# A linear-attention stage: u's turned rows get a tile of their own and are read back in the turn that wrote them

## The chip, the cores and the metric

The kernel runs on one core of one Trainium2 chip. The metric is device time in microseconds (us) of one execution, the median of several runs. Lower is better.

## The reference, cut to what matters

Four blocks in a row, each added to a residual x of shape (2, 2048, 256), fp32:

```python
x = x + attn_a(layernorm(x))      # gated scan
x = x + ffn(layernorm(x))         # 256 -> 1024 -> 256, ternary weights, gelu
x = x + attn_b(layernorm(x))      # the block that the change touches
x = x + ffn(layernorm(x))

# attn_b: 16 heads, q, k, v of 64 each, one step of the recurrence:
k_C  = k_t . C_QV                 # C_QV before this step
G    = G    + k_t (x) k_C
S_K  = S_K  + k_t (x) k_t
C_QV = C_QV + q_t (x) v_t
o_t  = q_t . (S_K . C_QV - G)
```

After the 2048 steps o is multiplied by W_o.

## The kernel before, in words

The program has three stages: `first_stage` (the gated scan), `feed_forward`, and `attention`, which also contains the last feed-forward (the D_ tiles) at its end. Every engine runs a fixed list of instructions written out by hand; semaphores order the engines against each other. There is no scheduler.

`attention` replaces the recurrence by a chunked form. The 2048 tokens of both batches are cut into 32 chunks of 64 tokens, and one pass of the loop `for j in range(CHUNKS)`, here called turn j, works on one chunk of all 16 heads and both batches. Turns run from 0 to 31. In a turn TensorE (PE) issues in this order:

- `by_states`, 128 products of 64x64 with the two running states (line 1261 with state_s, line 1265 with state_z). Batch 1 needs its bank back from the output of two chunks ago: it waits for `x_added`, the two adds of `add_out` on VectorE (DVE, line 1654).
- four projections of the next block (lines 256 to 258: q in even turns, k in odd ones). The first two need the banks of the masked scores free (`a_masked`).
- `o_by_scores` (1287) and `u_and_s` (1276). The latter reads k as rows (krow, `krow_done`) and the masked scores.
- `change_z` (1298) for chunk j-1. It reads u as rows (urow, `urow_done`).
- `values` (1240 to 1242), `scores_of` twice (1250: ut times q, then k times q for the next turn), and `out_product` of chunk j-1 (1310 to 1312).

The change is about the way of u from columns to rows. ScalarE (ACT) copies u to `ut`. DVE turns it in 32x32 blocks into the tile `turned` (`turn_u`, line 1627). SyncE's queue (SP) writes `turned` to a scratch tensor in device memory (`save_u`, line 1114) and reads it back in four transfers in another order of partitions into `landed` (`land_u`, line 1120). ACT copies it to `urow` (`store_u_rows`, line 1517). k takes the same way through its own tile k32 (`save_k`, `land_k`, `store_k_rows`), and so do the normalised rows of x, of which a block of 256 tokens of each batch is needed every fourth turn (turns 4, 8, ..., 24, and once each in turns 28 and 29 for the last feed-forward): `sp_move` writes `turned_x` (line 190), waits, and reads it back (line 193).

Before the change `turned` is not a tile of its own. It lies in `sc_a`, the place of the masked scores:

```python
turned = sc_a.rearrange("p m h t -> p (m h t)").rearrange("p (t m d) -> p t m d", t=4, m=PAIRS)
```

so DVE may write the masked scores of turn j+1 into `sc_a` (`mask_scores`, line 1610) only when the write of u has ended, and waits for that (`u_saved`). On DVE's list, `mask_scores` of turn j+1 is followed by `add_out` of chunk j-1, which PE's `by_states` waits for.

All of these transfers are issued by SP, which does them strictly in the order of its list: a wait holds up everything behind it. In the names of the trace `sc_and_k` holds `sc_a` and krow, `k` or `k_75` is k32, `C_turned` is `turned_x`, `ln_xn` is where the normalised rows land.

Of the kernel before, what the change touches and what calls it, by code (L numbers as in the profile page):

```python
# [13 lines left out]
P = 128  # L14
# [22 lines left out]
def hybrid_kernel(nc, x_d, gamma_d, wqkva_d, wq_d, wk_d, wv_d, wo_d, w1_d, b1_d, w2_d, b2_d, out_d):  # L37
# [12 lines left out]
    with outer:  # L50
# [83 lines left out]
        class LayerNorm:  # L134
# [49 lines left out]
            def sp_move(self, sp, slot, tile, count):  # L184


                if count:
                    sp.wait_ge(self.rows_landed, 64 * count)
                sp.wait_ge(self.rows_turned, 2 * (count + 1))
                sp.dma_start(rows_dram["x"], tile.rearrange("p g n f -> p g (n f)")).then_inc(self.rows_saved, 16)  # L190
                sp.wait_ge(self.rows_saved, 16 * (count + 1))
                for g in range(4):
                    sp.dma_start(self.xn[g * 32:(g + 1) * 32, slot, :, :],
                                 rows_dram["x"].rearrange("(r p) g c -> g p r c", r=4)[g]).then_inc(self.rows_landed, 16)

# [779 lines left out]
        def attention(before):  # L975
# [20 lines left out]
            turned = sc_a.rearrange("p m h t -> p (m h t)").rearrange("p (t m d) -> p t m d", t=4, m=PAIRS)  # L996
# [76 lines left out]

            def u_cols(p, what, n=1):

                return slice(p % 4 * P + what * CHUNK, p % 4 * P + (what + n) * CHUNK)
# [33 lines left out]
            def sync(sp):  # L1110
# [21 lines left out]
                def save_u(j):  # L1132
                    if j:
                        sp.wait_ge(u_landed, 64 * j)
                    save_turned(rows_dram["u"], turned, u_turned, u_saved, j)

                def land_u(j):
                    if j:
                        sp.wait_ge(urow_done, 2 * j)

                    sp.wait_ge(by_state_done, 2 * (j + 2))
                    land_rows(rows_dram["u"], landed, u_saved, u_landed, j)
# [3 lines left out]
                for j in range(CHUNKS):  # L1146
                    if j:
                        land_u(j - 1)
                    if j + 1 < CHUNKS:
                        save_k(j + 1)  # L1150
                        land_k(j + 1)
                    if j < LAST_STATE:
                        save_u(j)
                    if norm_of(j):
                        ln.sp_move(sp, norm_of(j) % 2, turned_x, chunk_moves(norm_of(j) - 2))
                    if block_of(j) is not None:
                        ln.sp_move(sp, block_of(j), turned_x, moves(block_of(j), 0))
                    if j == CHUNKS - 4:
                        sp.wait_ge(q_ready, 4 * KQ_BLOCKS)
                        sp.dma_start(w1t_again[:, :, :].rearrange("p a b -> p (a b)").bitcast(FP32), w1t_dram).then_inc(w1_loaded, 16)  # L1160
# [53 lines left out]
            def tensor(pe):  # L1214
# [181 lines left out]
                for j in range(CHUNKS):  # L1396
# [37 lines left out]
                    for x in range(2):  # L1434
# [15 lines left out]
                    if j:  # L1450
                        if j < LAST_STATE:
                            pe.wait_ge(s_added, 4 * (j + 1))
                        out_product(j - 1)

# [28 lines left out]
            def scalar(act):  # L1483
# [48 lines left out]
                def gelu(n):  # L1532
# [7 lines left out]
                    if n == 0:  # L1540
                        act.wait_ge(ln.rows_saved, 16 * (moves(1, 0) + 1))
                    nc.scalar.activation(hidden(n), bank[up_bank(n)][:, :], ACT.Gelu, bias=b1_sb[:, f:f + 1]).then_inc(gelu_done, 1)
# [15 lines left out]
                for j in range(CHUNKS):  # L1558
# [3 lines left out]
                    for x in range(4):  # L1562
                        if x == 3 and j:
                            store_u_rows(j - 1)
                        if not blk:
# [5 lines left out]
                    if j == 0:  # L1571
                        store_k_rows(j)
                    else:
# [32 lines left out]
            def vector(dve):  # L1606
# [17 lines left out]
                def turn_u(j):  # L1624
                    for b in range(B):
                        dve.wait_ge(ut_done, 4 * j + b + 3)
                        nc.vector.transpose(turned[:, 2 * b:2 * b + 2, :, :],
# [91 lines left out]
                for j in range(CHUNKS):  # L1719
# [33 lines left out]
                    if j + 1 < CHUNKS:  # L1753
                        dve.wait_ge(u_saved, 16 * (j + 1))
# [105 lines left out]
```

## Time and profile before

| | us |
|---|---|
| median of 3 runs | 1033.53 (1030.42 to 1037.01) |
| the profiled execution, its time | 1030.02 |
| its span | 1028.3 |
| PE busy | 984.2 (96%) |
| weight loads busy | 896.7 (87%) |
| DVE busy | 616.3 (60%) |
| ACT busy | 488.2 (47%) |
| POOL busy | 112.8 (11%) |

The page cuts the span in 40 slices. PE is at 8 or 9 tenths in nearly all of them, the granted clock of TensorE is at full speed in all slices but one (the eleventh, 257 to 283 us), and the DMA engines are busy 2 to 5 tenths of the time in the attention stage. The turns of the attention stage run from 236.5 us to 898.6 us of the span. A busy share of PE is an upper bound of its use, since matmuls overlap and their ends are modelled. A better reading is the length of one turn: every turn from 1 to 29 has the same list of matmuls in number and shape, so a turn that is longer than the shortest has lost the difference. In the waits, "PE bank L1261 <- DVE xres L1654: 12.2, 11, 2.5" means that PE sat idle before the matmuls of line 1261 for 12.2 us in all, 11 times, at most 2.5 us, and that DVE's add of line 1654 ended it.

### The profile page before, as it was taken

What the parts mean: (1) busy time and instruction counts of PE and PEld (TensorE: products, weight loads), DVE (VectorE), ACT (ScalarE), POOL (GpSimd) and SP (SyncE); (2) the same over time, 40 slices, a digit from 0 to 9 for tenths busy, and PEclk for the clock granted to TensorE, in tenths of its full rate; (3) what the DMA queues carried; (4) which work ended last, traced back from release to release, by engine and by line L of the source; (5) the groups of instructions that cost most, each with busy time, mean ns of one, the idle gap of its engine ahead of it and who ended that gap; (6) DMA issues with size and microseconds to landing.
All of it is one profiled execution on the core that took longest, in us unless ns stands there. A gap on an engine that the chain in (4) does not pass through costs nothing.

```text
span 1028.3 us, 41889 instructions
## 1 busy us (share of the span) xinstructions
PE 984.2 (96%) x18990; PEld 896.7 (87%) x18990; DVE 616.3 (60%) x1312; ACT 488.2 (47%) x941; POOL 112.8 (11%) x178
## 2 busy tenths in 40 slices
PE   8999899997999999999999999999999999989998
PEld 6888799997999889989989899899898987778997
DVE  7888887752446555556355546554644646566763
ACT  5676766643344434433443344334343335446663
POOL 2461332220000000000000000000000000032240
PEclk9999999999899999999999999999999999999999
DMA  9422211232233423332433332433342354222321
GB/s 316 151 61 82 83 62 62 83 142 87 92 98 126 147 91 120 130 123 92 139 126 106 128 124 85 146 111 100 126 146 85 106 166 156 95 73 92 124 73 52
DMA packets 76578, 115.84 MB, mean 113 GB/s; under 512 B 8816, under 2 KB 63472, under 8 KB 75376
## 3 DMA queue, kind: packets, MB, share of 16 engines
q1 hardware_dynamic: 76128, 113.15, 33.6%
q8 instruction: 150, 2.46, 1.0%
q14 instruction: 28, 0.23, 0.1%
q10 hardware_dynamic: 272, 0.00, 0.0%
HBM read 60.17 MB, written 52.95 MB: 110 GB/s over the span
## 4 chain that ended last, share of the span: by engine, by line
PE 70%; DMA 12%; DVE 9%; SPq 3%; ACT 3%; issue 2%; POOL 0%; POOLq 0%; DVEq 0%; ACTq 0%
PE bank L256 5%; DMA u_rows_scratch<-sc_and_k 5%; PE bank L257 5%; PE bank L258 5%; PE bank L1250 4%; PE bank L854 3%; PE bank L856 3%; PE bank L1261 3%; PE bank L1276 3%; DMA landed<-u_rows_scratch 3%; PE bank L1354 3%; PE bank L1355 3%; PE bank L837 3%; PE bank L836 3%; PE bank L1336 3%; DMA k_rows_scratch<-k 3%
## 5 line engine op out<-in xcount | busy, mean ns | idle before, releaser
L1620 DVE STREAM_TRANSPOSE k<-kt 128x512 f32<-128x512 f32 x64 | 43.2, 694 | 109.1 <-ACT kt L1488 105.7
L1488 ACT COPY kt<-bank 128x512 f32<-128x512 f32 x64 | 37.5, 586 | 135.5 <-PE bank L258 135.5
L1646 DVE TENSOR_TENSOR ot_lo<-bank,ot_hi 128x512 fp32r<-128x512 f32 x64 | 41.2, 686 | 94.4 <-ACT ot_hi L1511 93.9
L1493 ACT COPY qt<-bank 128x512 f32<-128x512 f32 x64 | 37.5, 586 | 112.8 <-PE bank L258 112.8
L1261 PE MATMUL bank<-qt,state_s 64*64 64x64 f32 x2048 | 73.8, 222 | 12.8 <-DVE xres L1654 12.2
L1261 PEld LDWEIGHTS bank<-qt,state_s 64*64 64x64 f32 x2048 | 66.8, 136 | 19.3 <-issue 14.2
L1498 ACT COPY v_all<-bank 128x512 f32<-128x512 f32 x64 | 37.6, 587 | 90.3 <-PE bank L1242 90.3
L1265 PE MATMUL bank<-qt,state_z 64*64 64x64 f32 x2048 | 74.3, 223 | 2.3 <-issue 1.2
L256 PE MATMUL bank<-ln_xhi,wk_hi 128*128 128x256 f32 x256 | 74.8, 292 | 1.7 <-DVE sc_and_k L1610 1.7
L1310 PE MATMUL bank<-wo_hi,ot_hi 128*128 128x256 f32 x256 | 74.7, 292 | 0.0
L256 PE MATMUL bank<-ln_xhi,wq_hi 128*128 128x256 f32 x256 | 74.3, 290 | 0.0
L257 PE MATMUL bank<-ln_xlo,wk_hi 128*128 128x256 f32 x256 | 73.1, 286 | 0.0
L258 PE MATMUL bank<-ln_xhi,wk_lo 128*128 128x256 f32 x256 | 73.0, 285 | 0.0
L257 PE MATMUL bank<-ln_xlo,wq_hi 128*128 128x256 f32 x256 | 72.6, 284 | 0.0
L258 PE MATMUL bank<-ln_xhi,wq_lo 128*128 128x256 f32 x256 | 72.6, 284 | 0.0
L1311 PE MATMUL bank<-wo_lo,ot_hi 128*128 128x256 f32 x256 | 71.4, 279 | 0.0
L1312 PE MATMUL bank<-wo_hi,ot_lo 128*128 128x256 f32 x256 | 71.4, 279 | 0.0
L1610 DVE TENSOR_TENSOR sc_and_k<-bank,causal 128x512 f32<-128x512 f32 x64 | 41.2, 686 | 48.6 <-DMA u_rows_scratch<-sc_and_k 38.2
L1265 PEld LDWEIGHTS bank<-qt,state_z 64*64 64x64 f32 x2048 | 66.3, 136 | 2.8 <-issue 2.5
L1610 DVE TENSOR_TENSOR sc_b<-bank,causal 128x512 f32<-128x512 f32 x64 | 41.2, 686 | 41.1 <-PE bank L1250 41.1
L1276 PE MATMUL bank<-sc_and_k 64*64 64x128 f32 (+1 forms) x2048 | 61.6, 268 | 3.5 <-ACT sc_and_k L1517 1.8
L856 PE MATMUL bank<-w2t,B_hid_lo 128*128 128x256 f32 x256 | 62.8, 281 | 0.0
(169 smaller groups left out, 2896.3 us busy)
## 6 DMA issues: line engine op xcount, KB each, us to landing
k_rows_scratch<-k SPq DMA_DIRECT2D x32, 512.0 KB, 3.5
k<-k_rows_scratch SPq DMA_DIRECT2D x128, 128.0 KB, 2.9
u_rows_scratch<-sc_and_k SPq DMA_DIRECT2D x31, 512.0 KB, 3.3
landed<-u_rows_scratch SPq DMA_DIRECT2D x124, 128.0 KB, 3.0
ln_xn<-x_rows_scratch SPq DMA_DIRECT2D x88, 128.0 KB, 2.9
x_rows_scratch<-B_turned SPq DMA_DIRECT2D x8, 512.0 KB, 2.6
x_rows_scratch<-C_turned SPq DMA_DIRECT2D x8, 512.0 KB, 4.8
out_dram<-xres SPq DMA_DIRECT2D x16, 256.0 KB, 3.1
```

Source lines behind the costliest of these rows:

```text
L256: nc.tensor.matmul(out, w_hi, x_hi, start=(k == 0), stop=False)
L257: nc.tensor.matmul(out, w_hi, x_lo, start=False, stop=False)
L258: return nc.tensor.matmul(out, w_lo, x_hi, start=False, stop=(k == last_k))
L856: last = nc.tensor.matmul(dst, hid_lo[:, b, f, c * P:(c + 1) * P], w2t[:, f, :], start=False, stop=(f == FC - 1))
L1261: last = nc.tensor.matmul(bank[UB[b][p // 4]][half(h), u_cols(p, 0)], state_s[half(h), b, p, :], qt[half(h), j // 2 % 2, p, j % 2, b, :], ...
L1265: last = nc.tensor.matmul(bank[OB[b]][half(1 - h), cols], state_z[half(h), b, p, :], qt[half(h), (j - 1) // 2 % 2, p, (j - 1) % 2, b, :], ...
L1276: last = nc.tensor.matmul(bank[UB[b][p // 4]][half(h), u_cols(p, 0, n)], krow[half(b), p, half(h)], sc_and_k[half(b), 0:n, p, h, :], start ...
L1310: nc.tensor.matmul(dst, ot_hi[:, p, :], w[0], start=(p == 0), stop=False)
L1311: nc.tensor.matmul(dst, ot_hi[:, p, :], w[1], start=False, stop=False)
L1312: last = nc.tensor.matmul(dst, ot_lo[:, p, :], w[0], start=False, stop=(p == PAIRS - 1))
L1610: nc.vector.tensor_tensor(to(h), bank[bank_of[h]][:, :].rearrange("p (m t) -> p m t", m=PAIRS), causal[:, None, :].to_broadcast([P, PAIRS, ...
L1620: nc.vector.transpose(k32[:, :, pairs, :], kt[:, pairs, j % 2, :, :].rearrange("p n b t -> p n (b t)") .rearrange("p n (t i) -> p t n i", ...
```

## The change

- `turn_u` writes u's turned rows of chunks 0 to 29 into a new tile `turned_u` at 96 KB, where nothing of the attention loop lay but `hidden_all`'s upper half, which is used from turn 30 on. Chunk 30 still uses the old place. `mask_scores` waits for `u_saved` only from turn 30 on. `turn_u` of chunk j waits instead for the write of chunk j-1, and the third gelu of the last feed-forward waits for the write of chunk 29.
- `land_u(j)` comes directly behind `save_u(j)` on SP's list, in turn j and not in turn j+1, and no longer waits for `by_states`.
- `sp_move` is cut in two. The write of the normalised rows goes ahead of `save_u` in its turn; the read-back goes to the head of the next turn. The load of w1t moves from the end of turn 28 to turn 29, behind that read-back.
- In turn 0, ACT copies k's rows before the last two copies of q instead of after them, and PE does the second half of `values` after the scores of turn 1 instead of before.

```diff
-            def sp_move(self, sp, slot, tile, count):
+            def sp_save(self, sp, tile, count):
                 if count:
                     sp.wait_ge(self.rows_landed, 64 * count)
                 sp.wait_ge(self.rows_turned, 2 * (count + 1))
                 sp.dma_start(rows_dram["x"], tile.rearrange("p g n f -> p g (n f)")).then_inc(self.rows_saved, 16)
+
+            def sp_land(self, sp, slot, count):
                 sp.wait_ge(self.rows_saved, 16 * (count + 1))
                 for g in range(4):
                     sp.dma_start(self.xn[g * 32:(g + 1) * 32, slot, :, :],
                                  rows_dram["x"].rearrange("(r p) g c -> g p r c", r=4)[g]).then_inc(self.rows_landed, 16)
...
-            turned = sc_a.rearrange("p m h t -> p (m h t)").rearrange("p (t m d) -> p t m d", t=4, m=PAIRS)
+            turned_again = sc_a.rearrange("p m h t -> p (m h t)").rearrange("p (t m d) -> p t m d", t=4, m=PAIRS)
+            turned_u = place("C_turned_u", 96, [P, 4, PAIRS, 32])
+            OWN_TILE = CHUNKS - 2
...
+            def turned(j):
+                return turned_u if j < OWN_TILE else turned_again
...
                 def land_u(j):
                     if j:
                         sp.wait_ge(urow_done, 2 * j)
-                    sp.wait_ge(by_state_done, 2 * (j + 2))
                     land_rows(rows_dram["u"], landed, u_saved, u_landed, j)
...
                 for j in range(CHUNKS):
                     if j:
-                        land_u(j - 1)
+                        if norm_of(j - 1):
+                            ln.sp_land(sp, norm_of(j - 1) % 2, chunk_moves(norm_of(j - 1) - 2))
+                        if block_of(j - 1) is not None:
+                            ln.sp_land(sp, block_of(j - 1), moves(block_of(j - 1), 0))
+                    if j == CHUNKS - 3:
+                        sp.wait_ge(q_ready, 4 * KQ_BLOCKS)
+                        sp.dma_start(w1t_again[:, :, :].rearrange("p a b -> p (a b)").bitcast(FP32), w1t_dram).then_inc(w1_loaded, 16)
                     if j + 1 < CHUNKS:
                         save_k(j + 1)
                         land_k(j + 1)
+                    if norm_of(j):
+                        ln.sp_save(sp, turned_x, chunk_moves(norm_of(j) - 2))
+                    if block_of(j) is not None:
+                        ln.sp_save(sp, turned_x, moves(block_of(j), 0))
                     if j < LAST_STATE:
                         save_u(j)
-                    if norm_of(j):
-                        ln.sp_move(sp, norm_of(j) % 2, turned_x, chunk_moves(norm_of(j) - 2))
-                    if block_of(j) is not None:
-                        ln.sp_move(sp, block_of(j), turned_x, moves(block_of(j), 0))
-                    if j == CHUNKS - 4:
-                        sp.wait_ge(q_ready, 4 * KQ_BLOCKS)
-                        sp.dma_start(w1t_again[:, :, :].rearrange("p a b -> p (a b)").bitcast(FP32), w1t_dram).then_inc(w1_loaded, 16)
+                        land_u(j)
...
-                    for x in range(2):
+                    for x in range(2 if j else 1):
                         if j:
                             pe.wait_ge(o_low, 2 * (j - 1) + x + 1)
                         values(j, x)
...
                         out_product(j - 1)
+                    else:
+                        values(j, 1)
...
+                    if n == 2:
+                        act.wait_ge(u_saved, 16 * OWN_TILE)
...
                         if x == 3 and j:
                             store_u_rows(j - 1)
+                        elif x == 2 and j == 0:
+                            store_k_rows(j)
...
-                    if j == 0:
-                        store_k_rows(j)
-                    else:
+                    if j:
                         high(j - 1)
...
                 def turn_u(j):
+                    if j:
+                        dve.wait_ge(u_saved, 16 * j)
                     for b in range(B):
                         dve.wait_ge(ut_done, 4 * j + b + 3)
-                        nc.vector.transpose(turned[:, 2 * b:2 * b + 2, :, :],
+                        nc.vector.transpose(turned(j)[:, 2 * b:2 * b + 2, :, :],
                                             ut[:, b, :, :].rearrange("p m (t i) -> p t m i", i=32)).then_inc(u_turned, 1)
...
                     if j + 1 < CHUNKS:
-                        dve.wait_ge(u_saved, 16 * (j + 1))
+                        if j >= OWN_TILE:
+                            dve.wait_ge(u_saved, 16 * (j + 1))
                         mask_scores(j + 1, lambda h: sc_a[:, :, h, :], AB, a_ready, a_masked)
```

DVE's list at the end of turn 5 and the start of turn 6, before. The names after "waits" are semaphores: C_usaved is `u_saved`, C_ut is `ut_done`, C_a is `a_ready`.

```order
L1627 STREAM_TRANSPOSE sc_and_k<-ut 128x512 [waits C_ut] x2
L1610 TENSOR_TENSOR sc_b<-bank,causal 128x512 [waits C_b] x2
L1701 TENSOR_TENSOR ln_xlo<-ln_xn,ln_xhi 128x4x64 [waits C_xhigh]
L1701 TENSOR_TENSOR ln_xlo<-ln_xn,ln_xhi 128x4x64
L1701 TENSOR_TENSOR ln_xlo<-ln_xn,ln_xhi 128x4x64 [waits C_xhigh]
L1701 TENSOR_TENSOR ln_xlo<-ln_xn,ln_xhi 128x4x64
L1610 TENSOR_TENSOR sc_and_k<-bank,causal 128x8x64 [waits C_a,C_usaved]
L1610 TENSOR_TENSOR sc_and_k<-bank,causal 128x8x64 [waits C_a]
L1654 TENSOR_TENSOR xres<-bank,xres 64x256 [waits C_out]
```

The same place in the changed kernel:

```order
L1647 STREAM_TRANSPOSE C_turned_u<-ut 128x512 [waits C_ut,C_usaved]
L1647 STREAM_TRANSPOSE C_turned_u<-ut 128x512 [waits C_ut]
L1628 TENSOR_TENSOR sc_b<-bank,causal 128x512 [waits C_b] x2
L1721 TENSOR_TENSOR ln_xlo<-ln_xn,ln_xhi 128x4x64 [waits C_xhigh]
L1721 TENSOR_TENSOR ln_xlo<-ln_xn,ln_xhi 128x4x64
L1721 TENSOR_TENSOR ln_xlo<-ln_xn,ln_xhi 128x4x64 [waits C_xhigh]
L1721 TENSOR_TENSOR ln_xlo<-ln_xn,ln_xhi 128x4x64
L1628 TENSOR_TENSOR sc_and_k<-bank,causal 128x8x64 [waits C_a] x2
L1674 TENSOR_TENSOR xres<-bank,xres 64x256 [waits C_out]
```

The wait for C_usaved has moved from the masked scores (sc_and_k) to the transposes that write the new tile, where it asks for the write of the turn before.

SP's list in turn 4 and the first half of turn 5, before. "landed" rows are the read-back of u, C_uturned is DVE's signal that u is turned, C_urow that ACT has copied the u rows before.

```order
L1114 DMA k_rows_scratch<-k_75 128x1024 [waits C_kturned]
L1120 DMA k_75<-k_rows_scratch 32x4x256 [waits C_ksaved,C_u]
L1120 DMA k_75<-k_rows_scratch 32x4x256 x3
L1114 DMA u_rows_scratch<-sc_and_k 128x1024 [waits C_uturned,C_uland]
L190 DMA x_rows_scratch<-C_turned 128x1024 [waits ln_rows_turned,ln_rows_landed]
L193 DMA ln_xn<-x_rows_scratch 32x4x256 [waits ln_rows_saved]
L193 DMA ln_xn<-x_rows_scratch 32x4x256 x3
L1120 DMA landed<-u_rows_scratch 32x4x256 [waits C_usaved,C_bystate,C_urow]
L1120 DMA landed<-u_rows_scratch 32x4x256 x3
L1114 DMA k_rows_scratch<-k_75 128x1024 [waits C_kturned]
L1120 DMA k_75<-k_rows_scratch 32x4x256 [waits C_ksaved,C_u]
L1120 DMA k_75<-k_rows_scratch 32x4x256 x3
```

The same stretch in the changed kernel:

```order
L1125 DMA k_rows_scratch<-k_75 128x1024 [waits C_kturned]
L1131 DMA k_75<-k_rows_scratch 32x4x256 [waits C_ksaved,C_u]
L1131 DMA k_75<-k_rows_scratch 32x4x256 x3
L189 DMA x_rows_scratch<-C_turned 128x1024 [waits ln_rows_turned,ln_rows_landed]
L1125 DMA u_rows_scratch<-C_turned_u 128x1024 [waits C_uturned,C_uland]
L1131 DMA landed<-u_rows_scratch 32x4x256 [waits C_usaved,C_urow]
L1131 DMA landed<-u_rows_scratch 32x4x256 x3
L195 DMA ln_xn<-x_rows_scratch 32x4x256 [waits ln_rows_saved]
L195 DMA ln_xn<-x_rows_scratch 32x4x256 x3
L1125 DMA k_rows_scratch<-k_75 128x1024 [waits C_kturned]
L1131 DMA k_75<-k_rows_scratch 32x4x256 [waits C_ksaved,C_u]
L1131 DMA k_75<-k_rows_scratch 32x4x256 x3
```

The write of x's rows stands ahead of the write of u, u's read-back directly behind its write and without the wait for C_bystate, and the read-back of x's rows after it. k's write of the next turn now follows x's read-back.

## Rows read from the trace of the kernel before

**Rows 1.** Busy time by stretch: turns 0, 1, 3, 2 to 28, 26, 29.
```profile
core 0: us, PE busy (x) PEld busy (x) DVE busy (x) ACT busy (x) POOL busy (x), PEclk, DMA share, GB/s
236.50:251.90 15.40, 13.11 (x361) 11.76 (x361) 6.61 (x12) 5.26 (x11) 0.00 (x0) 1.00 0.16 56
251.90:278.20 26.30, 22.92 (x536) 21.28 (x536) 10.30 (x18) 9.01 (x18) 0.00 (x0) 0.87 0.35 111
...
298.80:318.70 19.90, 19.90 (x537) 18.55 (x536) 11.65 (x27) 7.88 (x16) 1.22 (x2) 1.00 0.33 109
...
278.20:835.50 557.30, 542.26 (x14369) 504.17 (x14372) 303.03 (x624) 220.22 (x456) 9.68 (x16) 1.00 0.36 117
771.20:795.50 24.30, 21.75 (x533) 20.16 (x532) 10.85 (x20) 8.10 (x17) 0.00 (x0) 0.93 0.28 90
835.50:860.50 25.00, 21.56 (x534) 19.82 (x534) 13.62 (x26) 8.81 (x18) 0.00 (x0) 0.93 0.52 171
```

**Rows 2.** Waits of the whole span: total us, times, longest.
```profile
DVE sc_and_k L1610 <- DMA u_rows_scratch<-sc_and_k: 38.2, 29, 4.7
...
PE bank L1261 <- DVE xres L1654: 12.2, 11, 2.5
...
PE bank L1298 <- ACT kt L1488: 3.4, 1, 3.4
...
PE bank L1276 <- ACT sc_and_k L1517: 1.8, 1, 1.8
```

**Rows 3.** Waits of PE alone in turns 2 to 28.
```profile
PE bank L1261 <- DVE xres L1654: 11.9, 10, 2.5
PE bank L1298 <- issue: 2.2, 6, 0.7
```

**Rows 4.** Timeline of DVE, turn 4 into 5: start, us, instruction, idle before.
```profile
334.76 1.29 DVE L1610 TENSOR_TENSOR sc_b<-bank,causal 128x512 f32<-128x512 f32 x2 [1.13 <-PE bank L1250]
338.90 1.29 DVE L1610 TENSOR_TENSOR sc_and_k<-bank,causal 128x512 f32<-128x512 f32 x2 [2.85 <-DMA u_rows_scratch<-sc_and_k]
340.22 0.86 DVE L1654 TENSOR_TENSOR xres<-bank,xres 64x256 f32<-64x256 f32 x2
```

**Rows 5.** Timeline of SP's issues in turn 4 and the start of 5.
```profile
321.02 1.73 SPq L1120 DMA_DIRECT2D landed<-u_rows_scratch  x4
...
329.80 2.42 SPq L1120 DMA_DIRECT2D k<-k_rows_scratch  x4
333.70 0.34 SPq L1114 DMA_DIRECT2D u_rows_scratch<-sc_and_k  x1
334.14 0.39 SPq L190 DMA_DIRECT2D x_rows_scratch<-C_turned  x1
340.12 1.74 SPq L193 DMA_DIRECT2D ln_xn<-x_rows_scratch  x4
342.48 1.73 SPq L1120 DMA_DIRECT2D landed<-u_rows_scratch  x4
349.89 0.34 SPq L1114 DMA_DIRECT2D k_rows_scratch<-k  x1
```

**Rows 6.** Timeline of ACT in turn 4: the copy of u's rows.
```profile
325.95 1.14 ACT L1517 COPY urow<-landed 128x512 f32<-128x512 f32 x2
```

**Rows 7.** Chain of waits, turns 25 and 26: start, us, what.
```profile
761.14 3.80 DMA k_rows_scratch<-k
...
767.94 4.75 DMA u_rows_scratch<-sc_and_k
```

**Rows 8.** Chain of waits, turns 28 and 29.
```profile
830.98 5.39 DMA x_rows_scratch<-C_turned
...
841.76 6.30 DMA landed<-u_rows_scratch
```

**Rows 9.** Issues by line: count, KB each, median us to landing.
```profile
u_rows_scratch<-sc_and_k SPq DMA_DIRECT2D x31, 512.0 KB, 3.3
landed<-u_rows_scratch SPq DMA_DIRECT2D x124, 128.0 KB, 3.0
```

More of the change, by code:

```diff
@@ L194, in sp_move @@
                                  rows_dram["x"].rearrange("(r p) g c -> g p r c", r=4)[g]).then_inc(self.rows_landed, 16)
+            def sp_move(self, sp, slot, tile, count):
+                self.sp_save(sp, tile, count)
+                self.sp_land(sp, slot, count)
             def landed(self, slot, k):
@@ L1134, in save_u @@
                         sp.wait_ge(u_landed, 64 * j)
-                    save_turned(rows_dram["u"], turned, u_turned, u_saved, j)
+                    save_turned(rows_dram["u"], turned(j), u_turned, u_saved, j)
                 def land_u(j):
```

## The prediction

> **What bounds the kernel now.** I read the busy shares by stretch first, then the waits, then timelines of single turns, then the chain of waits where a turn was longest.
>
> TensorE is the busiest engine, and the stage to look at is the attention loop. Turns 1 to 29 have the same matmuls. Turn 3 takes 19.90 us, and PE is busy for all of it [rows 1]: this is the floor, set by PE's own work. Against it, turn 1 took 26.3, turn 29 took 25.0, and the 27 turns 2 to 28 together 557.3, where 27 x 19.9 = 537.3. The loss over the floor is 6.4 + 5.1 + 20.0 = 31.5 us, and turn 0 (shorter, with its own list) holds 15.40 - 13.11 = 2.3 us of idle PE [rows 1]. So at most some 34 us are to be had from anything done to the order of the attention loop, and everything else in the span is untouched by this change.
>
> What are these 31.5 us? DVE waited 29 times, 38.2 us in all, for the write of u out of the place of the scores [rows 2]. Most of that costs nothing. Where it does is seen at the border of turns 4 and 5 [rows 4]: the b scores are masked by 336.05, then DVE stands until 338.90, masks until 340.2, and only then adds the output (0.86 us, until 341.1). PE had finished the turn's list at 338.6 (318.7 + 19.9), ran batch 0 of by_states and then sat for the add. That is "PE bank L1261 <- DVE xres": 11.9 us in 10 of the turns 2 to 28 [rows 3], the largest wait that PE has in the loop. The write of u itself takes 3.3 us at the median [rows 9], but up to 4.75 where it shares the engines [rows 7].
>
> A second loss is SP's order. In a turn with normalised rows SP waits for their write, then issues their read-back (340.12), and only then u's (342.48) [rows 5]. In turn 25 this made u's rows late, ACT's next copy of k behind them late, so k's write late (761.14), and u's write went out only at 767.94 [rows 7], which is the 24.3 us of turn 26 at a clock of 0.93 [rows 1]. In turn 29 the write of x took 5.39, and u's read-back, behind x's and the load of w1t, 6.30, until 848.06 [rows 8]. PE waited 3.4 us in change_z, which wants the k copies that stand behind urow on ACT [rows 2].
>
> **The change, part by part.**
>
> *Own tile.* It adds no instruction on any compute engine. DVE's mask of the next turn's scores can start right behind its predecessor: at 336.05 instead of 338.90 in turn 4, so it ends at 337.3, and the add waits only for PE's out_product at 338.6, as in turn 3. In turns with chunk_low four operations more lie between the two masks; half of the 2.85 us that DVE idled in turn 4 would hold them, so the mask ends near the turn's end, at worst a tenth or two late. The new wait of turn_u asks for the write of the turn before, issued about 15 us into that turn and done 5 us later; the transpose comes 14 us after that, so nothing queues behind it. Gain in turns 2 to 28: the 11.9 us of waits at least [rows 3], the whole 20.0 at most. I take 13.8: the 11.9, and the 4.4 that turn 26 lost in place of the 2.5 that is its wait, because its rest is the slow clock behind the gap [rows 1, 3]. The other 6.2 us lie in turns with gaps in PE that no engine ended ("issue", 2.2 us by the modelled ends [rows 3]); the change does nothing for them, and I leave them.
>
> *Turn 29.* With u's read-back issued at the end of turn 28, ahead of x's and of w1t, its 6.30 us end some 5 us before they are wanted. Gain 25.0 - 19.9 = 5.1; bounds 3.4 (the wait alone [rows 2]) and 5.1.
>
> *Turns 0 and 1.* In turn 0 PE waited 1.8 us for krow, which ACT copied behind the last copies of q [rows 2]. The copy now goes ahead of those two; it fits if k's rows have landed by then, which no row here shows, and if not the 1.8 stays. The scores of turn 1 now come ahead of half of `values`, so their mask is done under it. Gain 2.3 in turn 0. Turn 1 loses its wait for the mask and the slow clock behind it (0.87 over the turn [rows 1]): 26.3 - 19.9 = 6.4, less 0.7 for an "issue" gap such as its neighbours have (longest 0.7 [rows 3]), 5.7. Bounds for both turns together: 1.8 (the krow wait alone) and 8.7.
>
> *SP's queue.* What is moved: 31 read-backs of u (4 issues each, 1.73 us of SP), 8 writes and 8 read-backs of x, one load of w1t; none is added. SP now stands at the end of each turn for u's write (3.3 to 5.4 us), with nothing behind it that is due: in turn 4, u's write would go at 333.7, be saved at 337 to 339, and the read-back be issued by 340 to 341. Next on the list are x's read-back (1.74) and k's write, which in odd turns was issued 11.3 us into the turn (349.89) [rows 5], and in even ones must be done before k's read-back, which was issued 11.1 us into turn 4 (329.80). ACT starts its copy of u's rows at 325.95, 7.3 us into turn 4, and had not waited [rows 6]. That is the deadline of the read-back: 19.9 + 7.3 - 15.0 = 12.2 us from u's write, and the two transfers with their issue are 3.3 + 1.8 + 3.0 = 8.1 us. Cost 0; if that cover is gone, each us beyond 12.2 costs one us of that turn. The Trainium skill, "DMA: Bandwidth & Descriptors", section "Rules for kernel authors", speaks against such an order: issue early, do the work, wait on the semaphore late. Section "Anatomy of one DMA" adds that the wait is spent on the issuing sequencer. By that rule SP's wait would be a cost in each turn; by the rows it falls in a stretch where SP has nothing to issue, and the sum goes by the rows.
>
> **Sum.** 2.3 + 5.7 + 13.8 + 5.1 = 26.9 us off the profiled execution's 1030.0: 1003.1. The median of the runs before is 1033.5, 3.5 above that execution, and their spread of 6.6 us is as wide as the stalls that go. With most of these gone I expect the median nearer to the profiled run than before, and say **1004**. The bounds of the terms give 17.1 (11.9 + 3.4 + 1.8) to 33.8, so 996 to 1013 by the profiled run.
>
> The clock: it was at its upper level, 1.00, in turn 3 and at 0.87 and 0.93 in the turns behind gaps of PE [rows 1]. The Trainium skill, "TensorE: Matmul & The Clock Gate", section "What's actually happening", has the throttled state as the default that activity releases. By that rule, the trace agrees, fuller turns can only keep the clock up.
>
> **The rivals.**
>
> *Part of it lost, 0.15: 1011 to 1018.* In the 8 turns with x's rows their write now goes out about 2 us ahead of u's and shares the engines with it. Rows for it: x's write took 5.39 right beside u's, and a read-back 6.30 beside the load of w1t [rows 8]. Then 5.4 + 1.9 + 6.3 = 13.6, 1.4 over the deadline, 8 times 11 us: 1014. Against it: 6.30 is one row in 124 issues with a median of 3.0 [rows 9], and its neighbour, the 1 MB load, is not there in seven of the eight.
>
> *Nothing, 0.05: 1026 to 1034.* The change would not do what it says if the add were late for another reason than the mask, such as chunk_low or the order of DVE's list. Then the same 11.9 us return, and DVE's idle time moves to another name. Against it: in turn 3, without such lateness, PE lost nothing.
>
> *Slower, 0.04: up to 1073.* SP's blocking wait becomes the bound: u's write and read-back chained in one queue, in each turn, beside k's and x's, take the worst of the rows each time: 5.4 + 2.9 + 6.3 = 14.6 us, 2.4 beyond the deadline. ACT's copies of k and ut stand behind urow, so PE loses it in all 29 turns, 70 us: 1003 + 70 = 1073. It decides from 12.2 us on, costs the gain from 13.1 on (26.9 / 29 = 0.9), and is slower by 1% from 13.5 on. Against it: the medians add to 8.1 [rows 9].
>
> **Chances.** The forecast, 996 to 1011, has 0.76. About 1%, or 10 us, is what a measurement of this kernel can tell. Faster by over 1% (below 1023) takes both: 0.90, since the part-lost case could reach that far in one case of a hundred. Within 1%: 0.06. Slower: 0.04. The range 996 to 1015 takes in the bounds of the terms and the nearer part of the second case, and leaves out less than 2 in 10.
>
> **What the profile after would show.** DVE's wait for u's write gone but for turn 30 to 31; PE's wait for the add below 1 us in all; turns 2 to 28 at 539 to 545 us; turns 1 and 29 below 21; the clock at 1.00 in all of them; SP's read-back of u issued within 0.1 us of the end of its write, near the turn's end; ACT starting urow without a wait. I would be wrong if ACT waited for `landed`, if PE's gaps called "issue" grew by as much as the waits shrank, or if the turns had a new floor above 20.

## The result, and the profile after

The changed kernel takes 1007.14 us (median of 3 runs, 1006.32 to 1007.17) against 1033.53. The ratio is 0.9738, with a 95% interval of 0.9697 to 0.9778. Run once more beside the experiments it gave 1008.47 us (1006.34 to 1010.83) and a ratio of 0.9766 (0.9726 to 0.9806). The forecast was 1004, with a range of 996 to 1015. The spread of the runs went from 6.6 us (3 runs) to 0.9 (3 runs); in the second set it is 12.3 before (11 runs) and 4.5 after (6 runs). The kernel before is the one whose time varies, and its clock varies with it: in the second set its runs of 1025.6 to 1028.0 us have a mean granted clock of 0.993 to 0.997, those above 1034 one of 0.989 to 0.991; the changed kernel's have 0.996 to 0.999.

The profiled execution after took 1007.17 us (span 1005.5) against 1030.02 (span 1028.3): 22.8 us less, where the sum of the prediction had 26.9.

The chain of waits of the whole span, by engine, after (before it read PE 70%, DMA 12%, DVE 9%):

```profile
PE 92%; DVE 3%; ACT 1%; issue 1%; DMA 1%; POOL 0%; SPq 0%; POOLq 0%; DVEq 0%; ACTq 0%
```

DMA's share of that chain went from 12% to 1%. The same stretches as in [rows 1], after: turns 0, 1, 3, 5, 2 to 28, 29, and 30 with 31.

```profile
core 0: us, PE busy (x) PEld busy (x) DVE busy (x) ACT busy (x) POOL busy (x), PEclk, DMA share, GB/s
236.70:249.80 13.10, 13.10 (x357) 11.59 (x356) 7.63 (x14) 4.70 (x10) 0.00 (x0) 1.00 0.34 119
249.80:271.80 22.00, 20.28 (x533) 18.72 (x532) 9.01 (x17) 9.50 (x19) 0.00 (x0) 1.00 0.32 106
291.90:311.80 19.90, 19.90 (x536) 18.54 (x535) 11.55 (x27) 7.88 (x16) 1.22 (x2) 1.00 0.32 105
331.70:351.60 19.90, 19.90 (x536) 18.55 (x535) 11.11 (x22) 9.09 (x20) 0.00 (x0) 1.00 0.45 136
271.80:816.70 544.90, 540.90 (x14368) 503.24 (x14367) 301.45 (x624) 219.46 (x456) 9.68 (x16) 1.00 0.37 120
...
816.70:836.80 20.10, 20.05 (x534) 18.60 (x533) 13.67 (x26) 8.90 (x18) 0.00 (x0) 1.00 0.62 212
836.80:876.20 39.40, 35.91 (x939) 29.81 (x940) 21.49 (x38) 20.60 (x40) 0.00 (x0) 1.00 0.35 109
```

Turn 0 lost its 2.3 us of idle PE, turn 29 fell from 25.0 to 20.1, turns 2 to 28 from 557.3 to 544.9, and the clock is 1.00 in all of them. The floor is the same 19.90. Turn 5, which before had waited for the add, is now at the floor, and turn 26 takes 20.5 (24.3 before). Turn 1 kept 2.1 us over the floor, and turns 30 and 31 together take 39.4, where they took 38.1. (Turn 31 is counted up to the end of its attention work.)

DVE at the border of turns 4 and 5 (columns as in [rows 4]):

```profile
327.88 1.29 DVE L1628 TENSOR_TENSOR sc_b<-bank,causal 128x512 f32<-128x512 f32 x2 [1.13 <-PE bank L1264]
329.09 1.28 DVE L1628 TENSOR_TENSOR sc_and_k<-bank,causal 128x512 f32<-128x512 f32 x2
331.82 0.86 DVE L1674 TENSOR_TENSOR xres<-bank,xres 64x256 f32<-64x256 f32 x2 [1.45 <-PE bank L1326]
```

The second mask follows the first without a gap, where it stood 2.85 us in [rows 4], and now DVE waits for PE (out_product, L1326) before the add. SP in the same turn (columns as in [rows 5]):

```profile
322.92 2.14 SPq L1131 DMA_DIRECT2D k<-k_rows_scratch  x4
325.16 0.38 SPq L189 DMA_DIRECT2D x_rows_scratch<-C_turned  x1
326.83 0.34 SPq L1125 DMA_DIRECT2D u_rows_scratch<-C_turned_u  x1
331.81 2.57 SPq L1131 DMA_DIRECT2D landed<-u_rows_scratch  x4
334.42 1.85 SPq L195 DMA_DIRECT2D ln_xn<-x_rows_scratch  x4
341.37 0.34 SPq L1125 DMA_DIRECT2D k_rows_scratch<-k  x1
```

Beside x's write, u's write takes until 331.8, 5.0 us, and SP stands for it. The read-back is issued over 331.81 to 334.38. ACT's copy of u's rows in turn 5 starts without a wait, behind its neighbour (338.49 + 0.59):

```profile
338.97 1.14 ACT L1533 COPY urow<-landed 128x512 f32<-128x512 f32 x2
```

Then SP has nothing to issue for 5 us, until k's write at 341.37. The waits of PE in turns 2 to 28, after, which answer to [rows 3]:

```profile
PE bank L1312 <- issue: 2.0, 5, 0.7
PE bank L262 <- issue: 1.0, 1, 1.0
PE bank L1254 <- issue: 0.3, 1, 0.3
PE bank L1264 <- issue: 0.3, 1, 0.3
PE bank L1275 <- issue: 0.2, 1, 0.2
```

The 11.9 us behind DVE's add are gone. What is left is called "issue", 3.8 us, where [rows 3] had 2.2; the second trace of the changed kernel has 6.3 us of it in this stretch. Over the whole span DVE waits for u's write once, in turn 30, where the old place is still used:

```profile
DVE sc_and_k L1628 <- DMA u_rows_scratch<-sc_and_k: 1.9, 1, 1.9
```

### The profile page after: what moved, and what is told of

Read it like the earlier page. It is cut to its first block, busy times and chain, and to the rows that moved or that the text cites. A ratio compares the mean times of both kernels' runs of the same rounds, so it can differ in the third digit from the quotient of the medians.

```text
span 1005.5 us, 41889 instructions
## 1 busy us (share of the span) xinstructions
PE 979.1 (97%) x18990; PEld 892.8 (89%) x18990; DVE 614.4 (61%) x1312; ACT 487.6 (48%) x941; POOL 112.8 (11%) x178
## 3 DMA queue, kind: packets, MB, share of 16 engines
q8 instruction: 150, 2.46, 1.0%
## 4 chain that ended last, share of the span: by engine, by line
PE 92%; DVE 3%; ACT 1%; issue 1%; DMA 1%; POOL 0%; SPq 0%; POOLq 0%; DVEq 0%; ACTq 0%
PE bank L262 7%; PE bank L1264 6%; PE bank L264 6%; PE bank L263 6%; PE bank L1290 5%; PE bank L1275 4%; PE bank L1254 4%; PE bank L1324 3%; PE bank L1301 3%; PE bank L860 3%; PE bank L862 3%; PE bank L1312 3%; PE bank L1255 3%; PE bank L1256 3%; PE bank L1279 3%; PE bank L1325 3%
## 5 line engine op out<-in xcount | busy, mean ns | idle before, releaser
L1666 DVE TENSOR_TENSOR ot_lo<-bank,ot_hi 128x512 fp32r<-128x512 f32 x64 | 41.2, 686 | 94.5 <-ACT ot_hi L1527 94.4
L1326 PE MATMUL bank<-wo_hi,ot_lo 128*128 128x256 f32 x256 | 71.4, 279 | 0.0
L1628 DVE TENSOR_TENSOR sc_b<-bank,causal 128x512 f32<-128x512 f32 x64 | 41.2, 686 | 41.6 <-PE bank L1264 41.6
L860 PE MATMUL bank<-w2t,B_hid_hi 128*128 128x256 f32 x256 | 62.7, 281 | 0.0
```

What stands on the lines that cost most here:

```text
L860: nc.tensor.matmul(dst, hid_hi[:, b, f, c * P:(c + 1) * P], w2t[:, f, :], start=(f == 0), stop=False)
L1326: last = nc.tensor.matmul(dst, ot_lo[:, p, :], w[0], start=False, stop=(p == PAIRS - 1))
```

## The experiments

Medians and ratios to the kernel before on the same chip, and the lengths of stretches read from each kernel's trace, in us. "t1" is turn 1. The rows were measured in several sets with a median of before of their own: 1033.5 (changed), 1032.6 (own tile only, SP's order only, turn 0 only, own tile and SP), 1034.6 (changed again, own tile and turn 0, x whole, read-back held) and 1029.0 (the last four). The changed kernel itself was not run in the sets of 1032.6 and 1029.0, so there the ratios and the traces compare better than the medians.

| kernel | median | ratio (95%) | t0 | t1 | t2-28 | t29 | t30-31 |
|---|---|---|---|---|---|---|---|
| before | 1033.5 | | 15.4 | 26.3 | 557.3 | 25.0 | 38.1 |
| changed | 1007.1 | 0.974 (0.970, 0.978) | 13.1 | 22.0 | 544.9 | 20.1 | 39.4 |
| changed again | 1008.5 | 0.977 (0.973, 0.981) | 13.1 | 20.6 | 547.8 | 20.1 | 40.0 |
| own tile only | 1015.9 | 0.984 (0.981, 0.988) | 15.4 | 21.8 | 547.1 | 24.4 | 39.7 |
| SP's order only | 1030.7 | 0.998 (0.995, 1.001) | 15.4 | 23.3 | 559.2 | 20.7 | 43.0 |
| turn 0 only | 1025.2 | 0.994 (0.992, 0.997) | 13.1 | 21.6 | 558.4 | 25.1 | 39.2 |
| own tile and SP | 1009.0 | 0.978 (0.974, 0.981) | 15.4 | 22.1 | 544.2 | 20.5 | 43.0 |
| own tile and turn 0 | 1013.7 | 0.981 (0.976, 0.986) | 13.1 | 21.5 | 546.5 | 25.2 | 40.2 |
| x whole, behind u | 1013.6 | 0.982 (0.978, 0.987) | 13.1 | 21.1 | 546.9 | 20.3 | 44.3 |
| read-back held | 1008.3 | 0.976 (0.972, 0.980) | 13.1 | 21.7 | 547.1 | 20.0 | 40.1 |
| one more write | 1018.3 | 0.989 (0.985, 0.993) | 13.1 | 21.5 | 548.0 | 19.9 | 45.0 |
| two more writes | 1109.2 | 1.077 (1.073, 1.082) | 13.1 | 22.3 | 632.2 | 20.4 | 55.4 |
| count shifted | 1019.3 | 0.991 (0.988, 0.994) | 13.1 | 20.5 | 546.9 | 20.4 | 39.5 |
| z inside values | 1018.1 | 0.989 (0.986, 0.993) | 13.1 | 21.2 | 553.4 | 20.2 | 41.2 |

**Changed again.** The changed kernel a second time, as the yardstick of its neighbours.

> The changed kernel once more, as the mark for the three beside it. 1005 to 1009, ratio to before near 0.974.

Measured 1008.5. Its trace has turns 2 to 28 at 547.8, 2.9 over the first, so a difference of 3 us in that stretch can't be told from none.

**Own tile only.** The kernel before with this and the waits that belong to it:

```diff
+            turned_u = place("C_turned_u", 96, [P, 4, PAIRS, 32])
...
-                        dve.wait_ge(u_saved, 16 * (j + 1))
+                        if j >= OWN_TILE:
+                            dve.wait_ge(u_saved, 16 * (j + 1))
```

> The kernel before with u's turned rows in a tile of their own and nothing else: SP's list and turn 0 stay. Theory (the mask's wait is most of the loss): TensorE's wait for the output add falls from 11.9 us to under 1 in turns 2 to 28, turn 26 falls from 24.3 to near 20, turn 29 keeps its 25 (u's read-back still stands behind x's and w1t's), turn 1 falls from 26.3 to near 22. That is 12 + 4 = 16 us: 1014 against a before of 1030. Rival (SP's order, that is the x transfers, makes the loss, and the wait of the mask is only where it shows): under 8 us gained, over 1022.

Measured 1015.9, and the turns as expected: turns 2 to 28 at 547.1 and turn 1 at 21.8, turn 29 still at 24.4. In its trace PE waits in turn 29 for ACT's k copies behind urow (2.8 us), as it did before, and in turns 2 to 28 no more for the add. Turn 29:

```profile
821.10:845.50 24.40, 21.60 (x536) 0.93 0.53 172
```

(Stretch, its length, PE busy, clock, DMA share, GB/s.) It gained 16.8 us against the 16 expected: the theory holds and the rival, under 8 us, falls. Turn 26, which the prediction put down to SP's order, takes 20.9 with the old order.

**SP's order only.** The kernel before with the new list of SP: the diff of the change above, its part in `sync`.

> The kernel before with the new list of SP alone: u read back behind its write, x's write ahead and its read-back a turn later; the mask still waits for u's write. Theory: turn 29 falls from 25.0 to near 20 and turn 26 loses half of its 4.4, the other waits for the output add stay: 5 to 8 us gained, about 1023. Rival (SP's order is the cause): over 15 us gained, 1015 or less. A second rival, that x's write ahead of u's makes the mask later, gives turns 5, 9, 13 and so on at 21.5 or more and no gain at all.

Measured 1030.7 with a ratio of 0.998 (0.995 to 1.001), no difference that can be told. Turn 29 gained as expected. Turn 26 did not lose half of its 4.4: it took 23.9, and PE waited 2.1 in it for the add. Turns 2 to 28 took 559.2, 1.9 us more than before, and turn 30 24.1, where before it took 19.5. Waits of the whole span in this kernel:

```profile
DVE sc_and_k L1619 <- DMA u_rows_scratch<-sc_and_k: 46.8, 28, 4.8
...
PE bank L1270 <- DVE xres L1663: 17.9, 12, 3.5
```

DVE's wait grew from 38.2 to 46.8 and PE's for the add from 12.2 to 17.9 [rows 2]: x's write goes out ahead of u's and makes it longer, and the mask still waits for it. In the eight turns with x's rows u's write takes 4.2 us on average, where it took 3.5, and 3.6 in the other turns of both kernels; of the 8.6 us that DVE waits longer, 7.7 are behind these eight writes. The second rival is right in this mechanism and wrong in its turns: 5, 9 and 13 kept their length within 0.1 us, and the one turn that PE pays for is 30 (24.1, with a wait of 3.5 for the add). Turns 16 and 20 got 1.8 and 1.9 longer, but they stand behind turns 15 and 19, which have no x write, and no run shows why. The losses, 1.9 in turns 2 to 28 and 4.9 in turns 30 and 31, nearly eat the gains of 3.0 in turn 1 and 4.3 in turn 29. My 5 to 8 us were too many.

I had not expected turn 1 to move:

```profile
252.20:275.50 23.30, 20.26 (x541) 1.00 0.40 129
```

PE waits 1.9 us for the mask in it, where it waited 1.7. What differs is the clock, 1.00 against 0.87 in [rows 1], and with it PE's own work, 20.26 us against 22.92: 2.7 of the 6.4 us that turn 1 had lost were the lower clock, which this kernel did not meet behind the same wait. The other 0.4 is a gap called issue.

**Turn 0 only.** Two edits:

```diff
-                    for x in range(2):
+                    for x in range(2 if j else 1):
...
+                        elif x == 2 and j == 0:
+                            store_k_rows(j)
```

> The kernel before with the two edits of turn 0 alone (k's rows copied earlier, half of values behind the scores). Theory: the 1.8 us wait for krow goes, u's write starts some 3 us earlier as SP is free sooner, so the mask of turn 1 is earlier by 3 and the slow clock behind it is partly gone: turns 0 and 1 together from 41.7 to 36 to 39, 3 to 6 us gained, about 1026. Rival (only the krow wait goes): 1.8 us, not to be told from none.

Measured 1025.2, 7.4 under the median of before in its set, ratio 0.994 (0.992 to 0.997). Turns 0 and 1 fell from 41.7 to 34.7, 1.3 more than the top of what was expected, with the mask still waiting for u's write. u's write was issued 10.5 us into turn 0 and not 14.9, and PE waited 0.2 us for the mask and not 1.7, at a clock of 1.00. So part of turn 1's loss hung on k's late rows in turn 0, which held up SP and with it u's write, and part on the lower clock behind it; the own tile alone gains as much (21.8).

**Own tile and SP's order, own tile and turn 0.** The changed kernel without one of its parts each.

> The changed kernel without its two edits of turn 0. Theory: as the changed kernel (about 1007) plus 2 to 3 us in turn 0; turn 1 already has its mask early. 1009. Rival (the parts overlap in turn 1, so that turn 0's edits carry none of it): the same as the changed kernel.

Measured 1009.0, 0.5 to 1.9 over the two medians of the changed kernel, which by itself does not tell the theory from the rival; the trace does: turn 0 costs the 2.3 us, turn 1 (22.1) nothing more than in the first trace of the changed kernel. The profiled execution, 1013.1, was the longest of six, and 3.6 us of it lie in turns 30 and 31 (43.0), which hold gaps called issue of 1.9 and 1.3.

> The changed kernel with the old list of SP: own tile and turn 0, but u read back in the next turn behind x's transfers. Theory: turn 29 keeps its 24 to 25 (4 to 5 us), and a few turns with x's rows lose some tenths: 5 to 7 us more than the changed kernel, 1012 to 1014. Rival (once the own tile has taken the mask's wait away, SP's order carries nothing): the same time as the changed kernel within 2 us.

Measured 1013.7, 5.2 over the changed kernel in the same set. Turn 29 took 25.2 (20.1), which is the whole difference. The rival, that SP's order carries nothing, falls. In turns 2 to 28 the old order costs nothing: 546.5 stands between the changed kernel's two traces, 544.9 and 547.8.

**x whole, behind u.** In SP's list of the changed kernel:

```diff
-                    if norm_of(j):
-                        ln.sp_save(sp, turned_x, chunk_moves(norm_of(j) - 2))
...
                     if j < LAST_STATE:
                         save_u(j)
                         land_u(j)
+                    if norm_of(j):
+                        ln.sp_move(sp, norm_of(j) % 2, turned_x, chunk_moves(norm_of(j) - 2))
...
```

> The changed kernel with x's write and read-back uncut and both behind u's read-back in their turn. Theory (what counts is that u's read-back does not stand behind x's): within 2 us of the changed kernel; x's rows land some 2 us later than now and nothing wants them before 15 us into the turn, but the first gelu of turn 30 waits for x's write, up to 1 us. Rival (cutting the move and writing x early is what helps): 3 to 5 us lost in the turns behind x's.

Measured 1013.6, 5.1 over the changed kernel, where the theory had up to 2. Turn 29 is as good as with the cut move (20.3), so u ahead of x is what serves there. The loss is in turn 30, 25.8 where the two traces of the changed kernel have 20.6 and 20.9, where I had named the reason and put it at up to 1 us:

```profile
ACT D_hidden L1555 <- DMA x_rows_scratch<-C_turned: 6.8, 1, 6.8
...
PE bank L1345 <- ACT D_hidden L1555: 3.8, 1, 3.8
```

The first gelu waits for x's last write, now issued behind u's whole way. No other turn with x's rows or behind one is more than 0.3 us over the longer of the changed kernel's two, so the rival holds for this one turn: the early write of x earns its place once, at the end of the loop.

**Read-back held.** The changed kernel with one line put back:

```diff
+                    sp.wait_ge(by_state_done, 2 * (j + 2))
                     land_rows(rows_dram["u"], landed, u_saved, u_landed, j)
```

> The changed kernel with the old wait for by_states put back in front of u's read-back, so that it is issued 2.4 us into the next turn and no longer in the same turn; the order of SP's list stays. Theory (the read-back has 2 to 4 us of cover): it lands at about 7.1 to 7.5 us where ACT wants it at 7.3, so 0 to 4 us lost in all, and a half us in some turns. Rival (reading back directly behind the write is what gains): 5 us or more lost.

Measured 1008.3 against 1008.5. ACT waited for u's rows 5.6 us in all, at most 0.7, and PE for none of it. That the read-back comes in the same turn gains nothing that can be told; its place in SP's list does.

**One more write, two more writes.** Ahead of u's write, the same rows to a spare scratch tensor (k is 1 or 2):

```diff
+                    for n in range(k):
+                        save_turned(rows_dram["spare"], turned(j), u_turned, u_spare, j)
+                        sp.wait_ge(u_spare, 16 * (k * j + n + 1))
                     save_turned(rows_dram["u"], turned(j), u_turned, u_saved, j)
```

> The changed kernel with u's turned rows written once more to a spare scratch tensor, and waited for, ahead of the write that is read back. In the changed kernel's trace the four read-backs of u have been issued 18.1 to 22.4 us after their turn's start, so they land at about 23 to 25.5, and ACT wants them at 27.2 (7.3 us into the next turn). Theory: 3.4 us more per turn fit mostly under this cover: 0 to 15 us lost, nothing in most turns. Rival (SP's blocking wait is a cost in each turn): 3.4 x 29 = 99 us lost. The 16 MB more that are written could cost something by themselves.

> The same with two more writes. Theory: 6.8 us more pass the cover of 2 to 4 us in every turn: 2.5 to 5 us lost in each of 29 turns, 70 to 145 us, and ACT waits for landed in every turn. Rival (no deadline near): under 20 us lost.

With one more, 1018.3: 10 to 11 us over the changed kernel by the medians, 0.013 to 0.016 by the ratios, and 6.4 by the two profiled executions (this kernel's was the shortest of its four runs). In the profiled one, turns 1 to 29 take 589.4 against 587.0 after, ACT waits for u's rows 8.8 us in all, at most 1.8, and turn 31, where the mask still waits for u's write, is 5.5 us longer. With two more, 1109.2, 102 over: turns 2 to 28 take 87.3 us more, 3.2 a turn, and in this kernel

```profile
ACT urow L1537 <- DMA landed<-u_rows_scratch: 112.3, 30, 7.4
...
PE bank L1316 <- ACT qt L1513: 46.6, 14, 5.5
```

27.3 of the 87.3 us are PE's own work, longer at a mean clock of 0.95 (busy 568.17 against 540.90); the rest is waiting. The first 3 to 4 us on SP's way are nearly free in turns 1 to 29 and the next are paid: the deadline is real, and I estimate from these two kernels and the 12.2 - 8.1 = 4.1 us of the prediction that the changed kernel is some 3 to 4 us away from it. The rival of the prediction that ended slower works as described, from about the point that it named, but the two transfers are not that slow.

**Count shifted.** 32 matmuls of 2 columns added to the warm-up at the start of the program:

```diff
+                    for n in range(32):
+                        nc.tensor.matmul(bank[WARM][:, 0:2], ident[:, :], ident[:, 0:2], start=True, stop=True)
```

> The changed kernel with 32 matmuls of 2 columns (64 instructions of TensorE) added to the warm-up at the very start. In both traces every gap of TensorE that no engine ended starts at instruction 193 or 194 modulo 256 of TensorE's own count. Theory (these gaps are instruction fetch, one block of 256 at a time): with the shift the gaps still start at 193 or 194 modulo 256, so at other turns and lines; change_z of turns 1, 11, 16, 17 and 21 is free of them and others have them; time within 4 us of the changed kernel. Rival (they belong to a place in the program, such as a bank or a late semaphore): the same lines in the same turns, and the count modulo 256 moves by 64.

I counted TensorE's weight loads, matmuls and semaphore instructions in the order of their start, from the first. In the changed kernel the 13 gaps of 0.15 us and more in turns 1 to 30 all begin at 193 or 194 modulo 256. In this kernel its 14 do so too, at other places. Turn 31 has one such gap in each, and others there end with a wait for DVE. My "every gap" was too much for the kernel before: the 0.5 us at the start of its turn 1 stand at 229, and one gap of 0.7 at 37 us, ahead of this stage, stands elsewhere in all of them. The shift was 128 instructions and not 64, since each of these matmuls stands as two in the trace. change_z of turns 1, 11, 16, 17 and 21 has no gap of this kind any more, and others have, as this one in turn 5, at instruction 8642 = 33 x 256 + 194:

```profile
354.94 0.28 PE L1314 MATMUL bank<-v_all,urow 64*64 64x64 f32 x4 [0.54 <-issue]
```

The rival falls: the gaps go with the count, not with the line. Turns 0 to 31 take 640.4 us, 639.5 in the changed kernel. By the traces the kernel is slower only by its start, where the added matmuls took 10.5 us and turn 0 begins 11.1 us later; the expected 4 us were a miss for that reason.

**z inside values.** change_z moved between the two halves of `values`:

```diff
                     for x in range(2 if j else 1):
                         if j:
                             pe.wait_ge(o_low, 2 * (j - 1) + x + 1)
                         values(j, x)
+                        if j and x == 0:
+                            pe.wait_ge(urow_done, 2 * j)
...
+                            change_z(j - 1)
```

> The changed kernel with change_z moved behind the first half of values. Before, o_by_scores, u_and_s and change_z make 768 instructions of TensorE in 4 us without a long matmul between them, and the gaps lie at change_z. Theory (fetch cannot keep up with this stretch): 12 long matmuls (1.5 us) between give it time, the gaps in change_z shrink by half: 2 to 4 us gained over the changed kernel, 1003 to 1005. DVE's turn of u stands behind the add of change_z and comes 1.5 us later, which the cover of 2 to 4 us of the read-back must carry; rival: it does not, ACT waits for landed in the turns with x's rows, and 2 to 5 us are lost.

The gaps in change_z are gone, as expected, but the kernel takes 1018.1, 10 us more than the changed one (13 to 16 by the ratios). The stretch of 64x64 products that I had put at 768 instructions in 4 us has 384 in 3.8 us: 64 products for each of the three, each with its weight load. Not by the rival: PE waits for no rows of u. Every turn from 2 to 29 has a new floor of 20.2 to 20.3 us:

```profile
270.70:824.10 553.40, 549.86 (x14368) 1.00 0.36 118
```

PE is busy for 9 us more with the same matmuls. In turn 3 the two halves of `values` take 3.17 us together where they took 3.00, change_z 1.09 (1.04), and the two groups ahead of them 2.84 (2.73). I take it that two more changes between products of 64x64 and of 128x512 cost this, but nothing here measures such a change alone. No version that I tried beats the changed kernel.

## Why the prediction was right

**What bounds the kernel** was read rightly: TensorE's own 19.90 us a turn, and the 31.5 us over it as all that there is to gain. After the change turns 1 to 29 lose 9.9 us over the floor (11.4 in the second trace).

**Own tile: 13.8 forecast for turns 2 to 28, 12.4 measured** (557.3 to 544.9), 9.5 to 12.4 over the two traces of the changed kernel. The mechanism is shown three times: the add's wait gone in the changed kernel, gone with the tile alone, and larger with SP's order alone. It was right to leave the "issue" gaps out of the gain; that they grew from 2.2 us to 3.8 and 6.3 is about what is missing, and the second trace, 547.8, lies beyond the 539 to 545 that I had named. The account of turn 26 was wrong in its cause: I called it a loss of SP's order, but it stays at 23.9 with the new order alone and falls to 20.9 with the tile alone. The sum had it under the tile, so no number suffered.

**Turn 29: 5.1 forecast, 4.9 measured,** and shown to belong to SP's order: 24.4 and 25.2 without it, 20.1 to 20.7 with it.

**Turns 0 and 1: 2.3 and 5.7 forecast, 2.3 and 4.3 measured.** With 22.0 turn 1 missed the "below 21" that I had named. Of the 1.4 that are missing, 1.0 is that it has two gaps, of 1.0 and 0.7, where I had allowed 0.7. The second trace of the changed kernel has turn 1 at 20.6, as forecast. What I had not seen is that the parts overlap there: each of them alone brings turn 1 down from 26.3, turn 0's edits to 21.6, the own tile to 21.8, and SP's order to 23.3, the last mostly through the clock (1.00 against 0.87, at the same wait for the mask). k's rows had landed in time for the earlier copy, which no row had shown.

**Turns 30 and 31: nothing forecast, 1.3 lost.** They hold gaps called issue of 0.6, 1.1 and 0.9, all at 193 or 194 (below), and a wait of 0.5 for the add, where before had gaps of 0.8 and 0.9 and a wait of 0.3.

**SP's queue: cost 0 forecast, none found.** SP stood 5 us for u's write in turn 4 and PE noticed nothing. The Trainium skill, "DMA: Bandwidth & Descriptors", section "Rules for kernel authors", asks to wait late; holding the read-back back to 2.4 us into the next turn (1008.3 against 1008.5) shows that under this cover it makes no difference either way. But I misjudged one part: the write of x ahead of u makes u's write in the turns with x's rows 4.6 us on average, where it was 3.5 (in turn 4 it was already 5.2 before and is 5.0 now). The own tile covers this; without it, it eats what the order gains.

**The sum** was 4.1 us too high by the profiled executions and 0.5 too high by the medians (26.4 gained). The median of before lies 3.5 over its profiled run and that of after on it, as the prediction expected of a kernel with fewer stalls. That the two nearly cancel is luck: the terms themselves fell short in turns 1, 2 to 28, 30 and 31.

**The rivals.** "Part of it lost" did not come: ACT did not wait for u's rows behind the x transfers. "Nothing" is excluded by the time and the trace. "Slower" has its deadline confirmed by the added writes, not reached by the change.

## What to carry to other kernels

A tile that shares its place with another makes one engine wait for a transfer, and a third engine pays; giving it its own 4 KB in each partition was worth more than all the reordering of the queue, which without it gained nothing that could be told. Where a queue does things strictly in order, ask for each transfer when it is wanted, and put that with the nearest deadline first: being first in the list gained 5 us in one turn, being earlier in time gained nothing. A part that is only tested inside the whole can be credited with what another part gains as well; turn 1 fell to nearly the same length by either of two edits. Compare turns of the same work with the shortest of them; the difference bounds the gain before anything is built.

## What the runs showed of the hardware that I had not expected

TensorE's gaps that the profile calls issue, 0.15 to 1.3 us in turns 1 to 30 of the two traces of the changed kernel and the shifted one, begin at instruction 193 or 194 modulo 256 of its own count, also after a shift of the count by 128. They come in or right behind stretches where the 64x64 products are dense, such as by_states with 256 instructions in 2.2 us. The profile of the DMA queues has 150 packets of instructions with 2.46 MB, 16.4 KB each; 150 x 256 = 38,400, and TensorE's records in the changed kernel are 38,458. In the traces of the changed kernel and the shifted one every gap of turns 1 to 31 ends 1.2 to 1.6 us behind the end of one of these packets (14, 15 and 15 gaps), while the packets come 3.3 to 8.4 us apart. By this timing TensorE stands for its own instructions there. The Trainium skill, "Runtime: NRT & Kernel Launch", section "Instruction fetch mechanics", has the instruction memory refilled in blocks of 16 KiB, 256 instructions, and calls the cost of crossing one mostly hidden. The spacing of the gaps agrees with the block; in this kernel the cost is not hidden everywhere: the gaps of turns 1 to 30 add up to 5.7 us before, 7.1 and 8.8 after.

The 32 matmuls of 2 columns stand in the trace as 64 and take 10.5 us, 165 ns each. The clock was at its upper level for the first 3.7 us of them, then for 10.2 us at its lower one, though PE was busy all through; the changed kernel, with other matmuls there, has 1.00 in the same stretch. Why it fell is not shown. First the matmuls, then the two stretches (length, PE busy, clock, DMA share, GB/s):

```profile
6.43 10.54 PE L445 MATMUL bank<-ident 128*128 128x2 f32 x64
...
6.60:10.00 3.40, 3.40 (x32) 1.00 1.06 344
10.10:20.30 10.20, 10.20 (x51) 0.51 1.08 372
```
